# Small attentions: score units in pairs, row maxima sent off earlier, causal zeroing after the exponential on GpSimd

## The reference, cut to what matters

| stage | heads, key heads, head width | causal | batches of 256 rows |
|---|---|---|---|
| l2a, attention of layer 3 (differential: two score maps per head group) | 32, 8, 8 | yes | 8 |
| l2f, attention inside the feed-forward block of layer 3 | 16, 16, 16 | yes | 4 |
| l3a, attention of layer 4 | 16, 1, 16 | no | 4 |

```
scores = jnp.einsum('bhqd,bhkd->bhqk', q, k) * scale
probs = softmax(where(causal, scores, finfo.min))
out = jnp.einsum('bhqk,bhkd->bhqd', probs, v)
```

## Time and profile before

### The profile page before, as it was taken

How to read it: one execution, slowest core, us unless ns; L and a number is a source line. 1 busy time by engine, 2 the same in 40 slices (tenths; PEclk the granted TensorE clock), 3 DMA queues, 4 the chain that set the end, 5 groups by cost and what they waited for, 6 DMA issues and landing times. The chain is left out here.

```text
span 3244.8 us, 36291 instructions
## 1 busy us (share of the span) xinstructions
PE 2318.6 (71%) x13182; PEld 1520.0 (47%) x13182; DVE 1846.5 (57%) x3528; ACT 1086.2 (33%) x2191; POOL 781.9 (24%) x765
## 2 busy tenths in 40 slices
PE   4477873399996588875413678887899968785738
PEld 1233322156664577762301344445788845544424
DVE  6677876634345455534687734443455554495377
ACT  1334441344443244431022233333343434202422
POOL 0122220045553566551243000000222210000020
PEclk7655556699997799997755678888899987796879
DMA  2000000000000344430000000002000000000000
GB/s 94 0 1 1 1 1 18 13 11 19 19 13 25 109 150 159 148 128 30 4 35 0 32 3 3 3 3 85 1 1 1 1 1 2 15 25 1 2 31 13
DMA packets 31104, 97.64 MB, mean 30 GB/s; under 512 B 3920, under 2 KB 16720, under 8 KB 29648
## 3 DMA queue, kind: packets, MB, share of 16 engines
q1 hardware_dynamic: 29392, 91.12, 8.3%
q0 software_dynamic: 1536, 4.20, 0.4%
HBM read 83.31 MB, written 11.01 MB: 29 GB/s over the span
## 5 line engine op out<-in xcount | busy, mean ns | idle before, releaser
L1716 POOL TENSOR_SCALAR l0f_probs<-l0f_probs,l0f_tot 128x128 f32<-128x128 f32 (+1 forms) x256 | 190.9, 767 | 241.6 <-DVE l0f_tot L1682 241.6
L1285 DVE TENSOR_REDUCE l2a_a_max<-ps 128x6 f32<-128x768 f32 x128 | 120.5, 956 | 118.6 <-PE ps L1142 117.8
L1931 PE MATMUL ps<-l0f_xh,l0f_wh 128*128 128x256 f32 x480 | 147.6, 307 | 41.5 <-issue 31.7
L2044 POOL TENSOR_TENSOR l0f_wl<-l0f_raw,l0f_wh 128x1024 fp32r<-128x1024 f32 x60 | 141.8, 2375 | 32.0 <-ACT l0f_wh L1968 32.0
L1932 PE MATMUL ps<-l0f_xl,l0f_wh 128*128 128x256 f32 x480 | 139.0, 290 | 0.0
L1933 PE MATMUL ps<-l0f_xh,l0f_wl 128*128 128x256 f32 x480 | 138.9, 289 | 0.0
L1623 ACT ACTIVATE l0f_probs<-ps,l0f_neg 128x128 f32<-128x128 f32 (+1 forms) x256 | 104.5, 425 | 92.8 <-DVE l0f_neg L1672 92.8
L2868 POOL TENSOR_TENSOR l2x_probs<-l2x_probs,l2x_rc 128x512 f32<-128x512 f32 x64 | 66.6, 1041 | 265.0 <-DVE l2x_rc L2783 265.0
L612 POOL TENSOR_TENSOR l0x_y<-l0x_y,l0x_hc 128x512 f32<-128x512 f32 x64 | 79.8, 1268 | 202.9 <-DVE l0x_hc L603 202.9
L1931 PEld LDWEIGHTS ps<-l0f_xh,l0f_wh 128*128 128x128 f32 x480 | 95.1, 198 | 54.3 <-issue 42.3
L1541 PE MATMUL ps<-l0f_xT,l0f_slab 128*128 128x512 f32 x192 | 95.5, 625 | 33.0 <-DMA l0f_slab<-in_g_l0f 32.9
(11 more groups left out here) (779 smaller groups left out, 6110.0 us busy)
## 6 DMA issues: line engine op xcount, KB each, us to landing
l0f_raw<-in_e_l0f SPq DMA_DIRECT2D x60, 768.0 KB, 4.4
scratch_rows<-zero SPq DMA_DIRECT2D x1, 3840.0 KB, 18.9
l0f_xb<-scratch_rows SPq DMA_DIRECT2D x15, 256.0 KB, 4.8
scratch_results<-l0f_yb SPq DMA_DIRECT2D x15, 256.0 KB, 5.0
l0f_slab<-in_g_l0f SPq DMA_DIRECT2D x8, 448.0 KB, 3.9
l1f_raw<-in_w_l1f SPq DMA_DIRECT2D x1, 3072.0 KB, 10.3
l2f_ew<-in_e_l2f SPq DMA_DIRECT2D x8, 384.0 KB, 3.0
l3f_raw<-in_w_l3f SPq DMA_DIRECT2D x1, 2438.0 KB, 8.7
```

The lines of the kernel that those rows point to most:

```text
L1285: dve.tensor_reduce(M[:, 2 * half:2 * half + 2, j, :], src.rearrange("p a (c n) -> p a c n", c=NB_), AX.X, ALU.max).then_inc(*unit_max.tick())
L1716: last = pool.tensor_scalar(pr[:, u % 3, a, r], pr[:, u % 3, a, r], tot[:, u % 3, qt, a:a + 1], None, ALU.mult)
L1931: pe.matmul(out, hi, xh[:, j % 2, c, :], start=c == 0, stop=False)
L2044: pool.tensor_tensor(wl[:, n % 2, :], raw[:, n % 4, 0:1024], wh[:, n % 2, :].bitcast(F32), ALU.subtract).then_inc(*w_lo.tick())
```

## The change

1. Units are issued in pairs. The matmuls of both units for the first 128 queries come first, then those for the other 128, then (causal) the four mask matmuls of both. Both slots of the ring must be free before the pair starts.
2. Units take the steps up to LAST (8 in l2a, 4 in l2f and l3a), two a step, and rows comes in step LAST. In l2a that is from 10 to 8, in l3a from 6 to 4, in l2f it stays 4.
3. In a step weigh and back now come ahead of the units, on TensorE, ACT and DVE, and in the ring.
4. When causal, the mask matmuls of the scores are gone. POOL sets the entries of later keys in `probs` to zero after the exponential (`keep`, an affine_select on 128 x 512 or 128 x 1024), weigh waits for POOL in place of ACT, and weigh and back come one step later (LAG 2). POOL's copy for the turns (`spread`) now stands behind `keep` in its list.
5. `probs` has another order of axes, so that the part which POOL handles is one pattern.

```diff
+    LAST, LAG = max(NU // 2, NC - 4), 2 if causal else 1
...
     def units_at(s):
-        return [u for u in range(NU) if u * (NC - 2) // NU == s]
+        return [u for u in range(NU) if u // 2 * LAST // (NU // 2) == s]
...
+        uses += [("weigh", O, 0) for O in octet_at(n, LAG)] + [("back", O, 0) for O in octet_at(n, LAG + 1)]
         if 0 <= it - 1 < NB2:
-            uses += [("unit", it - 1, u) for u in units_at(s)] + ([("rows", it - 1, 0)] if s == NC - 2 else [])
-        uses += [("weigh", O, 0) for O in octet_at(n, 1)] + [("back", O, 0) for O in octet_at(n, 2)]
+            uses += [("unit", it - 1, u) for u in units_at(s)] + ([("rows", it - 1, 0)] if s == LAST else [])
...
-            def unit(b, u):
+            def pair(b, us):
...
+                for u in us:
+                    pe.wait_ge(*ring_free("unit", b, u))
                 for qt in range(2):
...
+                    for u in us:
+                        j, half = hs.units[u]
+                        for a in range(2):
+                            r = hs.rows(2 * half + a, K)
+                            last = pe.matmul(ring("unit", b, u)[:, a, at:at + w], QT[z][r, j, qt * P:(qt + 1) * P], KT[z][r, hs.kj(j), 0:w],
+                                             start=qt == 0, stop=not causal and qt == 1)
+                        if qt == 1 and not causal:
+                            last.then_inc(*unit_ps.tick())
                 if causal:
+                    for u in us:
+                        for a in range(2):
+                            diagonal = ring("unit", b, u)[:, a, :].rearrange("p (q n) -> p q n", n=S)[:, :, 0:P]
+                            last = pe.matmul(diagonal, k.identb, k.mask_qk.unsqueeze(1).to_broadcast([P, 2, P]), start=False, stop=True)
+                        last.then_inc(*unit_ps.tick())
...
-                if causal:
-                    for a in range(2):
-                        diagonal = ps[:, 4 + 2 * (n % 2) + a, :].rearrange("p (j n) -> p j n", n=w)[:, :, 0:P]
-                        last = pe.matmul(diagonal, k.identb, k.mask_kq.unsqueeze(1).to_broadcast([P, len(js), P]), start=False, stop=True)
...
-                pe.wait_ge(*weighed(SPO * (O + 1)))
+                pe.wait_ge(*(kept if causal else weighed)(SPO * (O + 1)))
...
+            def keep(n):
+                O, (kt, p) = n // SPO, hs.parts[n % SPO]
+                js, q = (slice(0, 4), slice(P, S)) if p is None else (slice(2 * p, 2 * p + 2), slice(0, P))
+                pool.wait_ge(*weighed(n + 1))
+                part = PT[:, O % 2, kt, js, :, q].rearrange("p j a s -> p (j a) s")
+                last = pool.affine_select(part, part, [[0, part.shape[1]], [1, P]], ALU.is_ge, 0.0, base=0, channel_multiplier=-1)
+                last.then_inc(*kept.tick())
...
+            for it, s in STEPS:
+                n = (it - 2) * NC + s
+                if causal and n >= 0:
+                    keep(n)
+                if it < NB2 and s < 2:
+                    spread(it, s)
```

More of the change, by code:

```diff
@@ L1124, in turn @@
                 last.then_inc(*turned.tick())
-            def unit(b, u):
-                z, (j, half) = b % 3, hs.units[u]
-                banks = ring("unit", b, u)
-                if u == 0:
+            def pair(b, us):
+                z = b % 3
+                if us[0] == 0:
                     pe.wait_ge(*t_sb(NT_ * (b + 1)))
-                pe.wait_ge(*ring_free("unit", b, u))
+                for u in us:
+                    pe.wait_ge(*ring_free("unit", b, u))
                 for qt in range(2):
@@ L1169, in score @@
                         last = pe.matmul(bank[:, i * w:(i + step) * w], KT[z][r, hs.kj(js[i]), kt * P:(kt + 1) * P],
-                                         QT[z][r, js[i]:js[i] + step, q0:q0 + w], start=i == 0, stop=not causal and i + step == len(js))
-                if causal:
-                    for a in range(2):
-                        diagonal = ps[:, 4 + 2 * (n % 2) + a, :].rearrange("p (j n) -> p j n", n=w)[:, :, 0:P]
-                        last = pe.matmul(diagonal, k.identb, k.mask_kq.unsqueeze(1).to_broadcast([P, len(js), P]), start=False, stop=True)
+                                         QT[z][r, js[i]:js[i] + step, q0:q0 + w], start=i == 0, stop=i + step == len(js))
                 last.then_inc(*scored.tick())
@@ L1205, in at_pe @@
                         turn(it, i)
+                for O in octet_at(n, LAG):
+                    weigh(O)
+                for O in octet_at(n, LAG + 1):
+                    back(O)
                 if 0 <= it - 1 < NB2:
-                    for u in units_at(s):
-                        unit(it - 1, u)
-                    if s == NC - 2:
+                    us = units_at(s)
+                    for i in range(0, len(us), 2):
+                        pair(it - 1, us[i:i + 2])
+                    if s == LAST:
                         turn_rows(it - 1)
-                for O in octet_at(n, 1):
+            for n in TAIL:
+                for O in octet_at(n, LAG):
                     weigh(O)
[L1213 to L1217, removed]
-                for O in octet_at(n, 2):
+                for O in octet_at(n, LAG + 1):
                     back(O)
@@ L1318, in at_dve @@
                     low(it, s)
+                for O in octet_at(n, LAG + 1):
+                    normalise(O)
                 if 0 <= it - 1 < NB2:
```

30 lines of the change are left out of this document (10 added, 20 removed).

## The result

The changed kernel takes **3306.94 us** (median of 4 runs, 3303.58 to 3310.43), the kernel before on the same chip 3245.12 (median of 4). The ratio is 1.0198, 95% interval 1.0185 to 1.0211. That is 63 us slower than the 3243.72 shown ahead, where 15 were forecast; it lies outside the range of 3212 to 3292. The profiled execution took 3303.58 (span 3302.3), 57 more than the one of before.

A forecast was written before the change was run, and what follows sets the result against it. TensorE bounded the kernel before; with pairs, reductions and copies would decide. l2a +0.6, l2f +10.4 and l3a +4.7 made +15.7 on 3246.41, 3262.1; that execution lay 2.7 above the median, so 3259 us, range 3212 to 3292.

The forecast's parts named there:

- the clock term: In l2a, time lost to more 1.2 GHz under the new mix of work: +1 us a batch, +7 in all.
- The walk: Step-by-step sum of an l2a batch with both slots needed per pair: 40.6 us at 2.4 GHz, 44.1 with some 1.2 GHz.
- The bound: In l2a, the clock's upper limit: all of the batch at 1.2 GHz, about +6 us a batch (50 us).
- rival 4: Clock stays at 1.2 GHz for most of the new l2a: batch about 50 us, +50 in all, 3294; chance 0.08.
- P0 to P7: In an l2a batch, from pair 0 to pair 7, with weigh, turns and back between: 25.1 us at 2.4 GHz.
- First and last batch of l2a: In l2a, eight pairs without scores between, less covered turns, +4.3 us; at the end, masks gone but later step, -1.
- l2f and l3a: Pairing lengthens both stages: l2f +10.4 us, with no matmuls run together, and l3a, which has no masks, +4.7.
- TensorE's busy time: In l2a, a sign: busy time falls from 317 to about 250 us while the stage stays near 380.
- POOL: Mask pieces on POOL stay hidden: 4.3 to 6.6 us an octet against about 10, taken at the copy's rate.
- Rival 2: Behind each batch's first score, the DMA wait no longer lowers the clock: -27 us, 3217; chance 0.19.
- Rival 1: TensorE's work decides after all, slots come free earlier and pairs flow: 3164 us; chance 0.08.
- 4.3 us a batch: In each l2a batch, TensorE work that goes with the 12 mask pairs of scores: 4.3 us.

The follow-up runs named there:

- experiment 4: The changed kernel with four unused 128x512 products ahead of every causal score, overwritten by it; 3286.46 us, ratio 1.0119.
- Experiment 6: The changed kernel (pairs) with 20 unused products (10 in l2f and l3a) in each batch's wait for the DMAs of the maxima; 3291.57 us, ratio 1.0142.
- experiments 5: The changed kernel with single units again and 20 unused products (10 in l2f and l3a) in each batch's wait for the DMAs; 3216.36 us, ratio 0.9903.
- Experiment 2: The kernel before with score masks off TensorE, `keep` on POOL and a lag of two steps; units, order and rows as before; 3241.48 us, ratio 0.9998.
- experiment 7: The kernel before with only the change's schedule (earlier rows, weigh and back ahead of units), single units, masks on TensorE; 3246.84 us, ratio 1.0009.

## Why the prediction was wrong, and where it was right

**The step that failed is the clock term**, "I take +1 a batch, +7, nearer to what l2a shows than to l3a". The walk without any clock was 40.6 us a batch, and the text had 3.5 for the stretch at 1.2 GHz and 1 for more of it. The seven batches were to be 2.7 us shorter in all; they were 32.2 longer (346.5 against 314.3), and that is the miss of l2a (+34.4 where +0.6 stood). The batch of the rows above took 51.2 us at a granted clock of 0.60, 10.6 over the walk's 40.6. At 1.00, with added products, it took 44.5 (experiment 4): at least 6.7 of the 10.6 are the clock. The other 3.9 are added products on the path or too low a walk; that is not shown. The bound, "all of it, about +6 a batch (50 us)", was the answer (the first six batches were 50.0 on average), and rival 4 (3294, chance 0.08) the nearest case.

Both rows that the prediction weighed were there, and it took the wrong one. The l2a of before kept its clock in steps where TensorE never stopped; l3a's 0.67 in the earlier trace rows and the start of l2a up to its first score, with a granted clock of 0.54 over 41.3 us and 1.2 GHz in the earlier trace rows, were where TensorE waited for DVE step by step. The new step is of the second kind, by the walk's own 1.7 us of waiting in 2.73. Experiment 4 shows that the clock lengthens l2a and is no mere companion. Experiment 6 shows both kinds of wait at work: filling the one for the DMAs gave back 18.9 us of l2a, and the clock stayed at 0.72.

That the clock was the step that failed does not make it the larger cost of pairing. By experiments 5 and 6 that is the chain of slots, some 37 of 54 us in l2a. The prediction had this part in its walk and set the saved TensorE work against it.

**The walk held as far as the rows can tell.** P0 to P7, rows, first score, next pair 0: at 2.4 GHz with the added products 27.6, 4.7, 9.0 and 3.1 (experiment 4), against 25.1, 4.5, 8.0 and 2.95 without them; in the change at 1.2 GHz 32.9, 6.8, 8.1 and 3.4. The plain pair was given as 3.24 at 1.2 GHz and took 3.35. DVE's start behind a pair, 0.86 at 2.4 GHz, was 0.87 (2038.16 to 2039.03), and the first eight matmuls of a pair take the time of four (0.80, as for one unit in the earlier trace rows).

**First and last batch of l2a:** +4.3 was predicted and +5.1 measured (46.4 us from the stage's start to the first score, against 41.3); for the end -1, measured -2.9 (24.6 to 21.7).

**l2f and l3a:** +10.4 and +4.7 predicted, +13.7 and +7.3 measured. The clock fell there too (0.78 to 0.68, 0.67 to 0.62), but that it is the remainder is not shown: in l2f experiments 4 and 6 raised it (0.82 and 0.71) and the stage became longer (135.0 and 133.9), and in l3a a rise to 0.70 gave 1.5 us (experiment 6).

**TensorE's busy time** was to fall from 317 to about 250 in l2a. It fell to 304, since a matmul at 1.2 GHz is busy for longer. Busy time is no measure of work where the clock differs.

**POOL:** the forecast was that it is hidden, and it is. The price taken, that of the copy (1.07 for 512 elements), was still too dear: 0.64 for 512 and 1.09 for 1024. The Trainium skill's 12 cycles an element for branching on data (GPSIMD Engine Reference, Performance versus the Vector engine) would be an estimated 5.1 us for 512 elements; the trace shows 0.64, so it does not apply to this operation.

**Rival 2**, that the wait for the DMAs no longer brings the clock down, assumed it would fall well under 3 us. It stayed at 4.2. **Rival 1** (3164) is refuted by TensorE's 59 us of waits ahead of pairs.

**A gain that the prediction counted and no run gave alone** is that of the score masks: "4.3 us a batch". Experiment 2 has the masks gone, the clock of l2a at 0.69 and the time unchanged. A forecast for that half of the change with the same sum would have been wrong too.

The Trainium skill says that TensorE's tiling speeds up the matmuls and not the emptying of PSUM (TensorEngine Tiling, Performance Considerations). The trace agrees: eight matmuls in 0.80 us, and a step that ends with two reductions of 0.91.

The Trainium skill also tells of a kernel with frequent short stops between groups of matmuls, as PSUM banks are cycled, whose clock goes back and forth (TensorE: Matmul & The Clock Gate, A second HAM failure mode: psum-queue depth-cycling). The trace agrees in kind: l2a after the change goes between both levels, at a granted 0.61. The page's own case and its cost are in no run here.

## What to carry to other kernels

With two slots, don't let one producer take both: alternate them, so that one fills while the other empties. Price a change that adds short waits to TensorE at both clocks, and take the level from the row whose *pattern of waits* is that of the new code, not from the stage that the code replaces. Taking work off TensorE can be worth nothing, and a few products that compute nothing can be worth a per cent. Add them one by one: with single units the second ahead of each score was already a loss. And to tell a clock from a chain, compare two kernels at a like clock, as experiments 5 and 6 do; the stage and the clock of one pair of traces can't separate them.

## What the runs showed of the hardware that was not expected

- More work, less time: 384 products more in l2a took its granted clock from 0.61 to 0.91 and the stage from 414.6 to 387.1 us.
- Less work, more time: with 48 matmuls fewer (and `keep` and the longer lag in the same edit) l2f went from 115.6 to 121.2 us, at 0.66 in place of 0.78.
- The same granted clock and 37 us apart: l2a with 20 products in each DMA wait took 358.3 us with single units (0.73) and 395.7 with pairs (0.72).
- Eight matmuls of 24 rows in four strips of the array took 0.80 us at 1.2 GHz and 0.50 at 2.4, as four in two strips did.
- An affine_select on POOL, in place, took 0.637 us for 128x512 and 1.09 us for 128x1024, where a copy of 128x512 took 1.07.
- Executions of one kernel differ by more than 0.2%: ten of experiment 7 lay over 0.7% (3234.10 to 3257.37), thirteen of the kernel before also (3230.84 to 3254.67), four of the change over 0.2%. The mean clock of the program goes roughly with it: 0.784 and 0.777 at the ends of experiment 7, 0.793 and 0.786 at those of the kernel before. Where in the program it differs is not shown.
